# The third layer's products of a graph network in 128 columns in place of 256

## The reference

```python
e = relu(ea @ ee_w1 + ee_b1) @ ee_w2 + ee_b2
msg = x[src] + e
h = (1.0 + eps) * x + segment_sum(msg, dst)
h = relu(ln(h @ w1 + b1, g1, be1))      # 256 -> 1024
h = relu(ln(h @ w2 + b2, g2, be2))      # 1024 -> 1024
y = h @ w3 + b3                         # 1024 -> 256, the third layer
out = relu(ln(x + y, bn_g, bn_b))
return layernorm(x + out)
```

## Time and profile before

| | |
|---|---|
| three runs | 1134.03, 1137.17, 1137.71 us; median 1137.17 |
| the profiled execution | 1134.93 us, of it a span of 1133.1 us from the first to the last instruction |
| TensorE (PE) | busy 1078.9 us, 95%, 5297 matmuls |
| TensorE's weight loads (PEld) | busy 891.2 us, 79%, 5297 loads |
| VectorE (DVE) | busy 987.5 us, 87% |
| GpSimd (POOL) | busy 804.2 us, 71% |
| ScalarE (ACT) | busy 687.0 us, 61% |

### The profile page before, as it was taken

How to read it: one execution, slowest core, us unless ns; L and a number is a source line. 1 busy time by engine, 2 the same in 40 slices (tenths; PEclk the granted TensorE clock), 3 DMA queues, 4 the chain that set the end, 5 groups by cost and what they waited for, 6 DMA issues and landing times.

```text
span 1133.1 us, 21237 instructions
## 1 busy us (share of the span) xinstructions
PE 1078.9 (95%) x5297; PEld 891.2 (79%) x5297; DVE 987.5 (87%) x2795; ACT 687.0 (61%) x1677; POOL 804.2 (71%) x840
## 2 busy tenths in 40 slices
PE   6999999999999999999889999999999999999996
PEld 4788777777777777777677888888888888888875
DVE  6999999999999999999977888888888888888865
ACT  3577777787777777667644455445544554554453
POOL 7777777777777777777677777777777777777610
PEclk9999999999999999999999999999999999999999
DMA  8557767767766656667877777777777777777620
GB/s 236 142 156 201 204 191 202 205 191 205 204 191 184 180 170 177 189 178 207 266 203 217 224 218 210 220 221 216 209 219 222 213 211 220 222 212 215 202 76 12
DMA packets 106088, 222.13 MB, mean 196 GB/s; under 512 B 20003, under 2 KB 57369, under 8 KB 106010
## 3 DMA queue, kind: packets, MB, share of 16 engines
q0 software_dynamic: 53408, 164.16, 50.9%
q1 hardware_dynamic: 52602, 57.11, 16.2%
HBM read 203.96 MB, written 17.23 MB: 195 GB/s over the span
## 4 chain that ended last, share of the span: by engine, by line
PE 63%; DVE 12%; POOL 10%; issue 9%; DMA 5%; ACT 1%; POOLq 0%; SPq 0%; DVEq 0%; ACTq 0%
PE ps_z L1405 27%; POOL raw L990 8%; PE ps_e L1128 7%; PE ps_s L1349 6%; PE ps_y L1405 6%; PE ps_sum L1133 4%; PE ps_sum L1135 4%; DVE msg L2182 4%; PE ps_tr L1474 3%; DVE oh L225 3%; DVE msg L2188 3%; DMA raw<-in_x,src_all 2%; PE ps_w L1228 2%; POOL grow L1051 1%; DMA grow<-table_dram,src_all 1%
## 5 line engine op out<-in xcount | busy, mean ns | idle before, releaser
L1051 POOL DMA_INDIRECT grow<-table_dram,src_all x401 | 390.1, 973 | 143.7 <-issue 118.3
L990 POOL DMA_INDIRECT raw<-in_x,src_all x399 | 379.6, 951 | 121.7 <-issue 102.8
L1405 PE MATMUL ps_z<-w_high,a 128*128 128x512 f32 x784 | 252.4, 393 | 0.5 <-DVE a L2545 0.5
L1128 PE MATMUL ps_e<-we,attr 65*128 65x256 f32 x832 | 225.1, 392 | 15.0 <-DVE msg L2188 12.5
L1133 PE MATMUL ps_sum<-msg,oh 128*128 128x512 f32 x464 | 227.3, 490 | 7.6 <-DVE msg L2188 7.1
L1677 ACT ACTIVATE msg<-raw,w_sb 128x256 fp32r<-128x256 f32 x416 | 193.1, 499 | 54.7 <-DMA raw<-in_x,src_all 47.4
L225 DVE TENSOR_SCALAR oh<-lane,rel 128x128 fp32r<-128x128 f32 x871 | 211.1, 302 | 17.3 <-DMA raw<-in_x,src_all 17.3
L1128 PEld LDWEIGHTS ps_e<-we,attr 65*128 65x128 f32 x832 | 152.5, 193 | 58.2 <-issue 34.7
L2182 DVE SCALAR_TENSOR_TENSOR msg<-raw,w_sb,msg 128x256 fp32r<-128x256 f32 x416 | 181.9, 474 | 8.3 <-ACT msg L1680 8.2
L1135 PE MATMUL ps_sum<-msg,oh 128*128 128x512 f32 x464 | 183.7, 396 | 0.0
L1908 ACT ACTIVATE aF<-ps_tr,be,g 128x128 f32<-128x128 f32 x392 | 149.9, 464 | 36.3 <-PE ps_tr L1474 34.2
(11 more groups left out here) (189 smaller groups left out, 1557.4 us busy)
## 6 DMA issues: line engine op xcount, KB each, us to landing
attr<-in_attrT SPq DMA_DIRECT2D x50, 192.0 KB, 3.9
raw<-in_x,src_all POOLq DMA_INDIRECT x416, 3.3
grow<-table_dram,src_all POOLq DMA_INDIRECT x401, 3.7
w_raw<-in_m_w SPq DMA_DIRECT2D x48, 128.0 KB
table_dram<-table SPq DMA_DIRECT2D x23, 256.0 KB, 2.9
attr<-in_attrT SPq DMA_DIRECT2D x24, 160.0 KB, 4.2
xs<-in_x SPq DMA_DIRECT2D x24, 128.0 KB
xTb<-in_xT SPq DMA_DIRECT2D x24, 128.0 KB, 2.6
```

Source lines behind the costliest of these rows:

```text
L990: pool.indirect_dma_start(out=raw[:, j, :], out_offset=None, in_=x, in_offset=bass.IndirectOffsetOnAxis(ap=src_all[:, q * TILES + j:q * TI ...
L1051: pool.indirect_dma_start(out=grow[:, j, :].bitcast(F32), out_offset=None, in_=table_dram, in_offset=bass.IndirectOffsetOnAxis(ap=src_all[ ...
L1128: mm = pe.matmul(ps_e[k % 3][:, (j - j0) * D:(j - j0 + 1) * D], attr[:, j * P:(j + 1) * P], we1[:, :], start=True, stop=True)
L1405: mm = pe.matmul(acc, left[a], right[b], start=False, stop=stop and a == 1, skip_group_check=True)
```

## The change

In layer3 each product of 256 columns is made as two products of 128 columns, over columns 0 to 127 and 128 to 255 of the same bank, with the same stationary operand. For each piece k the helper `three` is called twice: three products for the first 128 columns, then three for the second. The number of waits and signals stays. The last block's own code is not touched.

```diff
                     pe.wait_ge(a_ready[1], 2 * b + half + 1)
                     for k in range(half * KH // 2, (half + 1) * KH // 2):
-                        mm = three(ps_y[:, 0:D], [a_of(1, b)[:, a, k, :] for a in range(2)],
-                                   [w[:, k, :] for w in (w3_high, w3_low)], k == KH - 1)
+                        for n in range(2):
+                            cols = slice(n * 128, (n + 1) * 128)
+                            mm = three(ps_y[:, cols], [a_of(1, b)[:, a, k, :] for a in range(2)],
+                                       [w[:, k, cols] for w in (w3_high, w3_low)], k == KH - 1)
                     if half == 1:
                         mm.then_inc(y_done, 1)
```

## The result

| | before | changed |
|---|---|---|
| median | 1135.72 us | 1193.33 us |
| lowest to highest of 4 runs | 1134.03 to 1137.71 | 1191.38 to 1198.79 |
| profiled execution, span | 1134.93, 1133.1 | 1193.55, 1191.7 |

The ratio is 1.0514 (95% interval 1.0493 to 1.0535): 57.6 us slower by the medians, where 56.6 us more and a time of 1193 us were forecast.

What follows compares the result with a forecast made beforehand. TensorE was taken as the bound, each narrow product paying a 110 ns weight load: 2.42 us more for each of 24 blocks, 58.1, less 1.5 for a vanished stall, +56.6 us; forecast 1193 us, range 1186 to 1207.

Steps and rivals of the forecast that it cites:

- three places: Loads behind short matmuls: a block's transposes, the start of the third layer's second half, the first stage's edge-counting products; 109 to 110 ns apart.
- The lower bound of 57 ns: Distance between starts of two first-stage counting products; at that price a block would need 2.74 us, 0.12 less than before.
- The upper one, 120: Price per product if the 256-column stream's fixed part of about 10 ns stays under the load bound: 69.6 us in all.
- The stall at 1083: TensorE's wait for gathered rows near 1083 us should vanish as later sums give the gathers slack: -1.5 us.
- the one at 611: Similar TensorE wait at 611 us, forecast to stay because GpSimd's gathers into it shift with block 0's third layer.
- the pause: GpSimd's 3.23 us pause before 1064.16, beside block 21's third layer; if it moved with TensorE's loop exit, nothing comes back.
- The end: Block 23's third layer before the last transposes: 0.1 us of cover, so its added 2.4 us are exposed.
- The fixed part that stays: Rival: the load-bound stream costs 115 to 120 ns a product, by handover or queue; 1199 to 1205 us; chance 11%.
- the loads partly hidden: Rival: a stream of narrow products runs at 85 ns each, as two counting products suggest; 1163 us; chance 5%.
- the columns (57 ns): Rival: columns decide, loads hidden or repeated weights free, below 60 ns a product; 1134 to 1137 us, not slower; chance 4%.
- The clock rival: Half-idle array drops TensorE's clock to 1.2 GHz in the third layers, 220 ns a product, 185 us, near 1320; chance 2%.
- GpSimd's slack: GpSimd's wait for TensorE's window sums was to grow by 2.4 us in each round, to about 3.5.

## Why the prediction was right

**The bound.** TensorE without a wait in the steady rounds, so that what is added to its stream is added to the round: right, 2.45 us in each of 20 rounds.

**The price of a product.** 110 ns by the load, from three places with loads 109 to 110 ns apart. The stream has 112. By the round, 2.86 + 2.45 = 5.31 us for 48, where the sum had 5.28. The lower bound of 57 ns was rightly set aside: the record starts early and waits for its weights inside its length. The upper one, 120, did not come either. The load as the cause was argued from the trace and is now shown: 64, 128 and 192 columns over a full load cost 112 to 113 ns, 128 columns over half a load cost 60. The Trainium skill's rule, "LDWEIGHTS (loading the stationary operand)" in "TensorE: Matmul & The Clock Gate", gives an estimate of 107 ns for 128 columns of weights. It is a good first guess here, 5 ns below the 112 of this trace at a granted clock of 1.00.

**The count.** 24 blocks and not 25, 5873 matmuls: right. The sum by what was measured: 24 x 2.45 = 58.8, less 1.6 for the stall, 57.2 us, against 57.6 by the medians. Forecast were 58.1 - 1.5 = 56.6. That the median met the 1193 us within 0.4 us is in part luck: the same kernel's second median was 1196.64 us, and what moved it, the clock, was not in the sum.

**What gave time back.** The stall at 1083 vanished, as the runs with and without a split in block 21 show, and the one at 611 stayed. That the pause stays beside block 21's third layer was left open; it did. What causes the pause, no run here shows. The end was exposed as said, with 2.2 us in place of 2.4.

**The rivals.** The fixed part that stays (120 ns), the loads partly hidden (85 ns) and the columns (57 ns) are all refuted by the pace of 112 ns in a stream of 24. The first of them was also summed too high at its lower end: at 115 ns a block costs 5.52 us, which is 63.8 us more in all and not 66. The Trainium skill's 81 ns for a sustained stream of 128-column matmuls (same page, "Back-to-back issue gap") is not seen here for 4-byte weights in any run with a full load.

**Where it was wrong.** The clock rival was priced for every round and given 2%. In the steady rounds the clock held, as the forecast needed. But it fell in single places in part of the executions, and the argument against it, that TensorE kept 1.00 while busy only 4.73 of 9.5 us at the end, failed: the same place with narrow products lost its clock in the profiles of both kernels that had them there, and once with the 256-column ones. In the four outer blocks the time is some 2 us over the load's price by the medians, most likely for this reason, and the changed kernel's runs reach 8 us above its lowest. And GpSimd's slack showed at the wait for the plain sums, since by the kernel's code gathers from the fifth tile on wait for the whole block's sums; I had looked only at the longer of the two waits for TensorE in the list before.

## What to carry to other kernels

In a stream in which each matmul brings its own load, a matmul costs the longer of its load and its columns. Here a load of 128 columns of fp32 weights costs 0.112 us, whether 64, 128 or 192 columns run over it. From 256 moving columns on the columns decide: 119 ns for 256 and 228 ns for 512, which is some 0.42 ns a column and 11 to 13 ns more (60 and 114 ns for 128 and 256 columns over a load of 64, with 6 to 7 ns more). Splitting the moving side below 256 columns therefore buys nothing and adds a whole load for each part, even if the part repeats its neighbour's weights; read the price from the distance between weight loads, not from durations or from starts of matmuls. Behind a wait of TensorE its clock can fall, in these profiles mostly where narrow products followed, so look at the granted clock of those places in several executions before trusting one time.

## What the runs showed that was not expected

- The clock stayed low while TensorE had no gap at all: 13.7 us at 0.50 with TensorE busy 13.70 and its loads 13.12 us. Shortly before each of the ten falls at a third layer it had waited (0.25 to 1.2 us at blocks 0, 1 and 22, 1.7 us in the tail). Most often products of at most 192 columns followed the wait, and once those of 256.
- At the lower level the same product costs 0.213 us in place of 0.112: the load takes nearly twice as long, in step with the clock. A product of 256 columns costs 0.213 there as well, so there the split doubles the cost.
- A load that is hidden still costs a little: 256 columns take 119 ns over a load of 128 columns and 114 over one of 64 (one run).
- GpSimd pauses for 3.2 to 3.6 us in the round in which TensorE's loop ends, in both kernels, and no instruction in the trace releases it.
